# Routed two-expert FFN slots: weight loads issued between the third and fourth low half on GpSimd, and one relu ahead of the gated copy on ScalarE

## The reference

```
x = x + 0.5 * ffn(layernorm(x));  x = x + attention(layernorm(x));  x = x + 0.5 * ffn(layernorm(x))
ffn(x): xln = ln(x, ln1);  x1 = x + sigmoid(xln @ Wr) * (xln @ Wv) @ Wo;  state = xln @ Ws
        h = ln(x1, ln2);  winner = argmax over 3 of confidence * share * difficulty + affinity
        experts 0, 1: square(relu(h @ K[e])) @ V[e]        K 256 x 1024, V 1024 x 256
        expert 2:     (h @ W1) * sigmoid(state @ W2) @ W3
        out = x1 + out[winner] * scale
```

## Time and profile before

| | us |
|---|---|
| median of 3 runs | 1071.55 (1071.44 to 1072.36) |
| the profiled execution | 1073.81 |
| its span, first to last instruction | 1072.1 |
| mean granted TensorE clock, share of full speed | 0.93 |
| first FFN, slots (first K product to barrier) | 167 to 437 |
| second FFN, slots (first K product to end) | 803 to 1072 |

### The profile page before, as it was taken

The page is one execution under the profiler, slowest core; times in us unless marked ns, Lnnn a source line. Parts: engine busy times, 40 slices in busy tenths (PEclk is TensorE's granted clock), DMA queues, the critical chain, the costliest instruction groups (busy, mean ns, idle before and its releaser), DMA issues.

```text
span 1072.1 us, 20295 instructions
## 1 busy us (share of the span) xinstructions
PE 925.1 (86%) x6490; PEld 853.0 (80%) x6490; DVE 738.3 (69%) x1871; ACT 587.5 (55%) x1279; POOL 545.9 (51%) x656
## 2 busy tenths in 40 slices
PE   7998767979799997788998898888878889799997
PEld 6786657879799887777887787766667779799997
DVE  4679986668766665366776567689976778766663
ACT  3767746463555553256653555586646545455552
POOL 3445766575666666471122001157656476566664
PEclk8978988988899999899999999999979889899998
DMA  7323256354655443220111122204264355555542
GB/s 253 119 86 151 82 196 203 107 180 176 195 168 150 146 141 103 82 64 11 60 60 40 40 79 86 72 21 172 112 193 149 103 195 194 156 159 157 156 137 66
DMA packets 72975, 134.58 MB, mean 126 GB/s; under 512 B 7422, under 2 KB 54398, under 8 KB 72704
## 3 DMA queue, kind: packets, MB, share of 16 engines
q0 software_dynamic: 19232, 73.75, 20.6%
q1 hardware_dynamic: 53632, 59.42, 17.8%
HBM read 89.81 MB, written 44.64 MB: 125 GB/s over the span
## 4 chain that ended last, share of the span: by engine, by line
PE 19%; DVE 19%; issue 8%; POOL 5%; ACT 5%; DMA 2%; POOLq 2%; SPq 0%; DVEq 0%; ACTq 0%
PE bank L431 10%; PE banks4to L1995 3%; PE banks4to L431 2%; DVE state_gate L1467 2%; PE bank L2007 2%; DVE pT_lo L2285 1%; ACT p L2155 1%; POOL out_x L1672 1%; POOLq L1704 1%; DVE chunk_max L2275 1%; POOL attn_x L2383 1%; POOL hr_lo L1665 1%; DVE relu_squared L1469 1%; DMA kx_lo<-first_product_halves 1%; ACT pT_hi L2164 1%
## 5 line engine op out<-in xcount | busy, mean ns | idle before, releaser
L1665 POOL TENSOR_TENSOR hr_lo<-relu_squared,hr_hi 128x512 fp32r<-128x512 f32 (+1 forms) x144 | 178.7, 1254 | 110.5 <-ACT hr_hi L1043 61.3
L431 PE MATMUL bank<-v_hi,hr_hi 128*128 x544 | 161.2, 296 | 22.5 <-POOL hr_lo L1665 19.3
L431 PE MATMUL bank<-v_hi,hr_lo 128*128 x544 | 157.6, 290 | 0.0
L431 PE MATMUL bank<-v_lo,hr_hi 128*128 x544 | 157.3, 289 | 0.0
L1455 DVE TENSOR_TENSOR relu_squared<-relu 128x512 f32<-128x512 f32 (+1 forms) x108 | 100.4, 933 | 56.7 <-ACT relu L1017 35.3
L431 PEld LDWEIGHTS bank<-v_hi,hr_hi 128*128 128x128 f32 x544 | 108.1, 199 | 27.1 <-issue 27.0
L1043 ACT CAST hr_hi<-relu_squared 128x512 fp32r<-128x512 f32 (+1 forms) x36 | 21.4, 596 | 191.9 <-DVE relu_squared L1469 191.9
L431 PEld LDWEIGHTS bank<-v_hi,hr_lo 128*128 128x128 f32 x544 | 108.0, 199 | 0.1
L431 PEld LDWEIGHTS bank<-v_lo,hr_hi 128*128 128x128 f32 x544 | 107.6, 198 | 0.0
L1446 DVE TENSOR_TENSOR slot_zT_lo<-banks4to,slot_zT_hi 128x512 fp32r<-128x512 f32 (+1 forms) x68 | 42.0, 655 | 85.8 <-ACT slot_zT_hi L999 79.3
L1599 POOL DMA_INDIRECT routed_rows<-out_rows,row_index x64 | 65.5, 1023 | 48.0 <-DVE row_index L1199 32.7
(11 more groups left out here) (334 smaller groups left out, 3158.3 us busy)
## 6 DMA issues: line engine op xcount, KB each, us to landing
kx_hi<-first_product_halves POOLq DMA_DIRECT2D x36, 512.0 KB
kx_lo<-first_product_halves POOLq DMA_DIRECT2D x36, 512.0 KB
slot_z<-routed_rows SPq DMA_DIRECT2D x60, 256.0 KB
slot_row<-routed_rows SPq DMA_DIRECT2D x30, 258.0 KB
attn_x<-x_after_ffn SPq DMA_DIRECT2D x16, 256.0 KB, 2.8
attn_out<-x_after_ffn SPq DMA_DIRECT2D x16, 256.0 KB, 2.7
x_after_attention<-attn_out SPq DMA_DIRECT2D x16, 256.0 KB, 2.1
x_rows<-x_after_attention SPq DMA_DIRECT2D x8, 512.0 KB, 4.4
```

Of the source, the lines that this page charges most:

```text
L431: mm = pe.matmul(outv, w(pw), m(pm), start=(n_first and k == 0), stop=(n_last and k == 2))
L1665: pool.tensor_tensor(b.hr[j % 2][1][:, 2 * q:2 * q + 2, 0:m], b.sq[n % 2][:, :, 0:m], b.hr[j % 2][0][:, 2 * q:2 * q + 2, 0:m].bitcast(F32) ...
```

## The change

No instruction is added or removed, except waits; work changes place in the hand-written orders.

- GpSimd: drain and `k_in(j+2)` now stand between `hrlo(j,2)` and `hrlo(j,3)`; `send(j-1)` follows `hrlo(j,3)`. The scatters of the last two groups come behind the sends, two tiles a slot in slots 2 to 5, and the pads in slot 5 instead of 6.
- ScalarE: `relu(j+1,0)` stands ahead of `gated(j)`; `h_hi(last-1)` ahead of `gated(0)`, `bd(last)` ahead of `relu(4,0)` and `gated(3)`. relu's first quarter has a wait on `hrhi` in every slot instead of slot 2 alone, and `relu(1,3)` has one.
- VectorE: `h_lo(last-1)` ahead of `sq(1,0)`, `late_starts` ahead of `orow(4)`, `rank(last)` behind `orow(3)`, `late_alone` at the end of slot 5's turn instead of in slot 6's.
- TensorE: `V(3)` ahead of `prefix(last)`.

```diff
--- before.py
+++ after.py
@@ -702,8 +702,8 @@
     slot.K(4, 1)
     slot.sT(5, 0)
     slot.sT(5, 1)
+    slot.V(3)
     r.prefix(last)
-    slot.V(3)
     for j in range(5, NSLOT):
         slot.K(j, 0)
         slot.K(j, 1)
@@ -1006,8 +1006,10 @@
             act.wait_ge(f["early"], 1)
         if j == EARLY_SLOTS:
             act.wait_ge(f["flag"], 1)
-        if j == 2 and n == 0:
+        if j and n == 0:
             act.wait_ge(f["hrhi"], 4 * j - 1)
+        if j == 1 and n == 3:
+            act.wait_ge(f["hrhi"], 4 * j + 2)
         if 4 * j + n >= 2:
             act.wait_ge(f["sq"], 4 * j + n - 1)
         for h in range(2):
@@ -1056,12 +1058,12 @@
     sigm(0)
     square(0, 2)
     relu(0, 3)
+    relu(1, 0)
+    r.h_hi(last - 1)
     gated(0)
-    relu(1, 0)
     square(1, 0)
     relu(1, 1)
     square(1, 1)
-    r.h_hi(last - 1)
     relu(1, 2)
     sigm(1)
     relu(1, 3)
@@ -1071,9 +1073,9 @@
     r.conf(last - 1)
     r.z2(last, range(GT))
     square(1, 2)
+    relu(2, 0)
     gated(1)
     for j in range(2, NSLOT):
-        relu(j, 0)
         square(j, 0)
         if j == 4:
             r.conf(last)
@@ -1088,9 +1090,10 @@
         if j + 1 < NSLOT:
             shi(j + 1, 0)
             shi(j + 1, 1)
+            if j == 3:
+                r.bd(last)
+            relu(j + 1, 0)
         gated(j)
-        if j == 3:
-            r.bd(last)
@@ -1494,8 +1497,8 @@
     r.rank(last - 2)
     sq(0, 2)
     gated(0)
+    r.h_lo(last - 1)
     sq(1, 0)
-    r.h_lo(last - 1)
     sq(1, 1)
@@ -1515,7 +1518,6 @@
         elif j == 5:
             r.late_places()
         elif j == 6:
-            r.late_alone()
             r.late_numbers()
@@ -1528,15 +1530,17 @@
             r.rank(last - 1)
         elif j == 4:
             r.win(last)
-            r.rank(last)
+        elif j == 5:
+            r.late_starts()
         orow(j - 1)
         if j == 3:
             r.bid_sum(last)
         elif j == 4:
+            r.rank(last)
             r.late_tiles()
         elif j == 5:
-            r.late_starts()
             r.late_regions()
+            r.late_alone()
@@ -1691,20 +1695,18 @@
     for j in range(2, NSLOT):
         hrlo(j, 0)
         hrlo(j, 1)
-        if j == 3:
-            tail.scatter(last - 1, range(0, 2))
-        elif j == 4:
-            tail.scatter(last - 1, range(2, GT))
-        elif j == 5:
-            tail.scatter(last)
-        elif j == 6:
-            tail.pads()
         hrlo(j, 2)
-        hrlo(j, 3)
         pool.drain()
         if j + 2 < NSLOT:
             tail.k_in(j + 2)
+        hrlo(j, 3)
         send(j - 1)
+        if j in (2, 3):
+            tail.scatter(last - 1, range(2 * j - 4, 2 * j - 2))
+        elif j in (4, 5):
+            tail.scatter(last, range(2 * j - 8, 2 * j - 6))
+        if j == 5:
+            tail.pads()
     send(NSLOT - 1)
```

## The result

| | before | after |
|---|---|---|
| median of the runs, us | 1071.95 (4 runs, 1071.44 to 1075.52) | 1033.05 (4 runs, 1031.61 to 1038.65) |
| profiled execution / its span | 1073.81 / 1072.1 | 1032.55 / 1030.9 |
| mean granted TensorE clock | 0.930 | 0.943 |

The ratio is 0.964, with a 95% interval of 0.960 to 0.968: 38.9 us less, and the forecast was 1033.5. The sum came out; not all of its terms did, and the change has a cost that had been priced at nothing.

A forecast was written before the change was run, and what follows sets the result against it. GpSimd's round of 13.46 us was taken to bound the slots. Terms 7.9 + 8.5 + 5.4 + 1.7 + 8.0 + 6.5 = 38.0 off 1073.81 gave 1035.8, less 2.26 for the median: 1033.5 us, range 1026 to 1050.

The forecast's parts named there:

- What bounds the kernel: Slots 8 to 16: GpSimd's round of 13.46 us sets the period; it becomes TensorE's 12.34, gaining 7.9 and 8.5.
- Ring of 11.44: GpSimd's round in steady slots after the change: 11.44 us, or 11.6 with relu(j+1,0) fully ahead of the copy.
- Slack of quarter 3: Before V(j) in a TensorE-bound round: quarter 3's result is there at 17.8 of 18.9 us, 1.1 to spare.
- Slot 16 to 17: No kx_lo wait and clock staying up: 11.7 us free pace, gaining 1.7 in the first FFN, 5.4 in the second.
- Early slots: Slots 0 to 7: earlier bids and an earlier slot 7 gain 6.5 in the first FFN, 8.0 in the second.
- Slot 7 still waiting for VectorE, 2 to 4 us: Sign expected in the profile after: TensorE's slot 7 still waits 2 to 4 us for VectorE.
- Just not the bound: Slot 8's rows, loaded after the pads land, come at about 919 and do not set slot 8's start.
- The relu ahead of the gated copy: ScalarE's relu(j+1,0), 1.01 us, ahead of the copy: copy at 7.7 in the round, ring 11.6, below TensorE's 12.34.
- Rival 1: Steady slots: VectorE and GpSimd hinder each other more, ring 12.5 to 13, 8 us less gain: 1042; chance 0.17.
- Rival 2: Early slots give nothing, VectorE's table and the pads setting slot 8 as before: 1048; chance 0.14.
- Rival 3: Quarter 3, 0.86 later behind the weights, delays V(j) in each of 32 slots: 1085; chance 0.06.
- Rival 4: More than forecast: clock dips go too and slot 8 starts 4 us earlier still in each FFN: 1026; chance 0.08.

The follow-up runs named there:

- the fastest kernel: The kernel after with relu(j+1,0) put back behind gated(j) from slot 1 on: 1028.40 us, ratio 0.9593 to the kernel before.

## Why the prediction was right, and where not

- **What bounds the kernel.** Right: GpSimd's round set the slot period. Moving one line of its order, alone, took 13.3 to 12.34, TensorE's own work, and 8 slots to 98.2 where 98.3 were forecast. Both terms, 7.9 and 8.5, stand to 0.1 in the profiled executions.
- **Ring of 11.44.** At most 11.83 measured, 0.48 of it the wait for the copy behind relu(j+1,0) (the step had 11.6 for that case). Less than 12.34 either way.
- **Slack of quarter 3.** "1.1 of slack" before `V(j)` holds: above, quarter 3 ends at 931.59 and V(9) starts at 933.60, which less 0.8 leaves 1.2. (One of its terms, 1.8 for twelve products 0.12 apart, is 1.4 by its own figures; relu(10,0) starts 1.64 behind slot 10's first product.) What the step missed is the ring through the `sq` buffers, with about 1.5 left. It made no difference here; with 2.65 more, the expectation worked out of the step was a period of 12.85, and it was 13.41.
- **Slot 16 to 17.** 5.8 and 2.0 for 5.4 and 1.7: 11.4 each where the free pace was put at 11.7. The 5.4 is in part luck. It holds 3.75 for the fallen clock, which the old order has in two of eight stretches. That loss may also be part of the 2.26 by which the profiled execution stood above its median; the forecast took off both. Whether it is, no run shows.
- **Early slots.** 5.8 + 7.5 = 13.3 for 14.5 in the profiled executions. By timed runs and without the relu, GpSimd's order alone against the fastest kernel, the early moves bring 15.0, with an interval of some 4.5. So the sum was near, but its parts were shared out wrongly. The earlier `h_hi` and `h_lo`, put at 5.3, are worth 4.0 in the traces and 7 in the runs, and 5.3 lies within what both vary by. V(3) ahead of the prefix was to start a chain worth 9.2; beside the rest of the change nothing of it can be told. GpSimd's places of scatters and pads bring 4 to 5. VectorE's pieces at 0 are not contradicted. "Slot 7 still waiting for VectorE, 2 to 4 us" was the sign, and the wait, 3.06, stands before slot 6. "Just not the bound", of slot 8's rows, was right in the kernel after; in the fastest kernel TensorE waits for them. Its timeline of TensorE, second FFN:

```profile
889.19 1.38 PE L766 MATMUL banks4to<-ident_sb,slot_z 128*128 128x128 f32 x8 [1.86 <-DMA slot_z<-routed_rows]
```

- **The relu ahead of the gated copy, priced at 0 beyond its place in the ring.** Wrong: it costs 4.65 us with the rest of the change, 11 without the early moves, and 4 in the old order of GpSimd. The step looked at a steady round and at whether the copy had slack there. It did not ask what the copy waits for in slot 16, where the next slot's first product comes later than the gate, and where the copy, put behind it, makes V(17) wait 2.9 instead of 1.5. That was to be had from the trace of before, where the gated copy of slot 16 stands 1.43 us ahead of slot 17's first product at 1054.73. Timeline of ScalarE, before:

```profile
1053.30 0.41 ACT L1043 CAST hr_hi<-relu_squared 128x256 fp32r<-128x256 f32 x1 [5.39 <-DVE relu_squared L1469]
```

- **Rival 1** (VectorE and GpSimd hold each other up): refuted for the new order, where quarter 3 takes 1.29 at 930.30; shown in the old order with the relu ahead, 1.85. By the Trainium skill (SBUF — State Buffer, Who interferes with whom) whichever of two such instructions issues first has the shared ports for its whole length, and the other is blocked. The trace agrees in kind, one of a pair being stretched in each case above; that the first keeps its time it doesn't show, since quarter 3's row at 978.67, which is stretched, starts 0.04 ahead of the square's.
- **Rival 2** (nothing from the early slots): refuted, 13.3 us in the traces. **Rival 3** (slower through the later quarter 3): refuted as put, 0.86 is inside the slack. But the kernel with the sends moved as well shows that its kind of loss, by the estimate above, lies only some 1.5 us farther on. **Rival 4** (more): it takes a kernel without the relu to come near its 1026.

The result stands partly on errors that cancel. Without the relu's cost the kernel is at 1028.4, 5 us below a forecast that had priced that cost at nothing. So other gains were left out as well: V(17) in the first FFN, where 4.17 us of waiting fall to 1.52 without the relu in front, as they do (to 1.48) with GpSimd's order alone, is one of 2.65 whose wait the trace of before showed.

## What to carry to other kernels

An engine that waits in a hole of its own round for someone else's result can do there what needs no result: here one line moved on GpSimd brought 2.7%. A time read from one profiled execution can hold a loss that the next doesn't have, as slot 16's fallen clock did; other traces with the same order show it. Before putting an operation ahead of a waiting one, look at every kind of round, the short last ones above all: an input that is always there in the steady state may be the last thing to arrive at the end. And draw the rings through every pair of buffers, not just along the queue that looks full: the one that closed when quarter 3 went 2.65 us farther ran through none of the waits that the trace of before showed.

## What the hardware showed that was not expected

Small operations can stand for very long beside GpSimd. The timeline of VectorE after, a 128 x 3 operation of the late table, beside two `hr_lo`, and busy time by stretch for TensorE's slot 6 behind it:

```profile
864.06 3.17 DVE L1281 SCALAR_TENSOR_TENSOR table_work_e<-table_work_e 128x3 f32<-128x3 f32 x1
```

```profile
869.00:872.00 3.00, 2.75 (x13) 2.75 (x14) 2.96 (x4) 0.00 (x0) 1.39 (x1) 0.50 0.01 3
878.50:889.00 10.50, 8.41 (x55) 7.80 (x54) 8.46 (x34) 3.96 (x9) 8.25 (x9) 0.83 0.60 232
```

The same operation takes 0.16 us in the trace of before, and 3.17 in both FFNs after. Its row starts during GpSimd's last scatter (863.68 to 864.65) and ends 0.04 us behind the second of the two `hr_lo` (864.67 to 867.19). VectorE's table is what TensorE then waits for (3.06 at 869.25), and behind that wait the granted clock is 0.50, the 1.2 GHz level, over 869 to 875: the products of `K` start 0.21 apart there instead of 0.12, so, as an estimate, some 2.5 of these 6 us are lost too. GpSimd's own row scaling (2.19 to 4.70) shows the same from the other side.

In V(5), at 878.5 to 889, TensorE pauses although the profile shows nothing that it waits for ("issue", 1.05 us at 886.38, and smaller ones), with a DMA share of 0.60. What makes these pauses was not tried. They differ between executions: slots 0 to 8 of the first FFN took 121.8 in the kernel after and 125.5 in the one that differs from it only at slot 17, with a mean granted clock of 0.94 and 0.89. So a term of the early slots that is read from a single profile is good to some 4 us, and the timed runs had to decide them, as far as their intervals allow.
